# One decoder layer on one core: two head groups' values in one bank, causal masks by 32x32 products, and projections with both weight halves side by side

## The reference, cut to what matters

```
def attn(x):        # 16 heads of 8 features, causal
    q, k, v = x @ Wq.T, x @ Wk.T * scale, x @ Wv.T
    qk = einsum('bthd,bshd->bhts', q, k);  qk = where(causal, qk, -inf)
    qkv = einsum('bsdh,bhts->bthd', v, softmax(qk))
    return layernorm(qkv, gamma, beta) @ Wo.T
def xattn(k, v, q): # one head, 64 context rows
    return softmax((q @ Wq.T + bq) @ (k @ Wk.T).T * scale) @ (v @ Wv.T + bv) @ Wo.T + bo
def ffn(x):         # 8 experts, all of them, weighed by entmax gates
    return sum_e gate_e * (relu(x @ W1[e] + b1[e]) @ W2[e] + b2[e])
x = x + attn(layernorm(x)); x = x + xattn(ctx, ctx, layernorm(x)); x = x + ffn(layernorm(x))
```

## Time and profile before

| | us |
|---|---|
| median of 3 runs | 703.99 |
| lowest and highest | 702.42, 704.47 |
| the profiled execution | 702.24 |
| its span, first to last instruction | 700.5 |

### The profile page before, as it was taken

The page is one execution under the profiler, slowest core; times in us unless marked ns, Lnnn a source line. Parts: engine busy times, 40 slices in busy tenths (PEclk is TensorE's granted clock), DMA queues, the critical chain, the costliest instruction groups (busy, mean ns, idle before and its releaser), DMA issues.

```text
span 700.5 us, 14922 instructions
## 1 busy us (share of the span) xinstructions
PE 677.0 (97%) x4858; PEld 491.3 (70%) x4858; DVE 458.7 (65%) x969; ACT 422.7 (60%) x810; POOL 359.4 (51%) x588
## 2 busy tenths in 40 slices
PE   5889999999999999999999999999999999999997
PEld 3455655777677776787777777787768767777775
DVE  3763577459954797369865796379845995565544
ACT  3348335875587547854676647854686458665453
POOL 6434144663466426564475437643576337554362
PEclk9999789999999999999999999999999999999999
DMA  4514200052006300260006200440006200600050
GB/s 141 194 32 113 91 2 19 8 133 91 3 19 138 109 3 17 54 169 21 17 1 153 90 2 17 104 140 2 17 20 146 78 2 3 142 14 1 16 120 16
DMA packets 35299, 43.03 MB, mean 61 GB/s; under 512 B 2738, under 2 KB 18750, under 8 KB 35262
## 3 DMA queue, kind: packets, MB, share of 16 engines
q1 hardware_dynamic: 35262, 42.55, 22.6%
HBM read 10.04 MB, written 2.10 MB: 17 GB/s over the span
## 4 chain that ended last, share of the span: by engine, by line
PE 77%; DVE 10%; issue 6%; ACT 5%; SPq 1%; DMA 1%; POOL 0%; DVEq 0%; ACTq 0%; POOLq 0%
PE h_ps L936 9%; PE y_ps L936 7%; PE h_ps L938 7%; PE h_ps L937 7%; PE y_ps L938 7%; PE y_ps L937 7%; DVE negmax L1507 4%; PE sbuf_s L1015 3%; PE sbuf_m L1029 3%; PE sbuf_s L1029 3%; PE sbuf_s L997 3%; PE sbuf_s L992 3%; PE sbuf_s L968 2%; DVE h_lo L1616 2%; PE sbuf_s L936 1%
## 5 line engine op out<-in xcount | busy, mean ns | idle before, releaser
L1616 DVE SCALAR_TENSOR_TENSOR h_lo<-h_ps,h_hi 128x512 fp32r<-128x512 f32 x256 | 174.2, 685 | 158.9 <-ACT h_hi L1340 157.7
L1340 ACT ACTIVATE h_hi<-h_ps 128x512 fp32r<-128x512 f32 x256 | 152.4, 599 | 111.0 <-PE h_ps L938 106.0
L807 POOL TENSOR_SCALAR_AFFINE_SELECT prob<-prob 128x512 f32<-128x512 f32 x128 | 80.0, 641 | 133.4 <-ACT prob L1321 131.0
L1507 DVE TENSOR_REDUCE negmax<-sbuf_s 128x4 f32<-128x1024 f32 (+1 forms) x96 | 113.3, 1218 | 12.0 <-PE sbuf_s L997 10.3
L936 PE MATMUL y_ps<-h_lo,w_hi 128*128 128x512 f32 x255 | 109.4, 429 | 3.4 <-ACT y_sb L1349 2.3
L936 PE MATMUL h_ps<-fT_lo,w_hi 128*128 128x512 f32 x256 | 110.9, 433 | 1.5 <-DVE fT_lo L1482 0.9
L1321 ACT ACTIVATE prob<-sbuf_s 128x768 f32<-128x768 f32 x128 | 99.5, 812 | 15.6 <-PE sbuf_s L1015 14.8
L938 PE MATMUL h_ps<-fT_hi,w_hi 128*128 128x512 f32 x256 | 101.2, 395 | 0.0
L937 PE MATMUL h_ps<-fT_hi,w_lo 128*128 128x512 f32 x256 | 101.1, 395 | 0.0
L938 PE MATMUL y_ps<-h_hi,w_hi 128*128 128x512 f32 x255 | 100.7, 395 | 0.0
L937 PE MATMUL y_ps<-h_hi,w_lo 128*128 128x512 f32 x255 | 100.7, 395 | 0.0
(11 more groups left out here) (412 smaller groups left out, 1136.0 us busy)
## 6 DMA issues: line engine op xcount, KB each, us to landing
gate_b<-gT SPq DMA_DIRECT2D x64, 256.0 KB, 4.9
stacks<-qk SPq DMA_DIRECT2D x48, 256.0 KB, 2.5
x_t<-in_x_dram SPq DMA_DIRECT2D x8, 256.0 KB, 2.8
gate_b<-in_L_ffn_W_dram SPq DMA_DIRECT2D x1, 2048.0 KB, 9.5
x_r<-in_x_dram SPq DMA_DIRECT2D x8, 256.0 KB, 4.0
out_dram<-sums SPq DMA_DIRECT2D x7, 256.0 KB, 4.4
prob<-in_ctx_dram SPq DMA_DIRECT2D x1, 512.0 KB, 4.1
prob<-in_L_ffn_b_dram SPq DMA_DIRECT2D x1, 512.0 KB
```

The source lines that it names most:

```text
L807: pool.affine_select(out=v, in_=v, compare_op=ALU.is_ge, fill=0.0, base=0, pattern=[[0, 2], [0, 2], [1, P]], channel_multiplier=-1).then_i ...
L1340: act.activation(h_hi[:, c % HB, :], h_ps[:, c % 2, :], ACT.Relu).then_inc(hhi_made, 1)
L1507: dve.tensor_reduce(negmax[:, tile, :].rearrange("p (j g) -> p j g", g=NG)[:, j:j + 2, gs], halves[buf].rearrange("p j (g s) -> p j g s", ...
L1616: dve.scalar_tensor_tensor(out=h_lo[:, c % HB, :], in0=h_ps[:, c % 2, :], scalar=0.0, in1=h_hi[:, c % HB, :], op0=ALU.max, op1=ALU.subtrac ...
```

## The change

It has four parts.

1. **Values.** `PV` takes two head groups (four steps a round instead of eight). The window of 32 value columns of the second group starts 16 columns earlier, so that its 9 used columns land 16 partitions further, and its products add to the first group's in the same bank (`values`). There are as many products as before. `attT` has half its columns, so each `BT` has 2 transposes instead of 4, and ACT has 4 copies a round instead of 8. `prob` has three buffers.
2. **Masks.** In rounds the identity product is done as 16 products of 32x32, one for each strip of rows and of columns, and touches only the 32x32 blocks on the diagonal: 128 or 64 columns. The blocks beyond it are masked by six more rows of `qs` and `ks`, which were idle in the 32-row stacks. POOL makes these rows (`cells`) and SP spreads them by 8 DMAs in phase 0, behind SC 15 and ahead of the second K (`spread_cells`). The products L992 carry them at their old size. Phase 0 keeps the old masks.
3. **Projections.** In rounds V and WO use `project_wide`: the activations' hi part by both weight halves side by side (256 columns), then the lo part by the weights' hi half (128 columns), 8 matmuls instead of 12. The two halves of the result are added when the bank is read: V by four reductions on DVE instead of one copy, WO by two additions instead of one. Phase 0 keeps the old form.
4. **Places.** All tables are laid anew, and `FILL` has 63 matmuls instead of 105: of these 22 instead of 45 stand in phase 0 from the first MAX of the second pair on. `pairs` on DVE moves from between MAX 9 and MAX 10 (dve=5.5) to behind MAX 11 (dve=6.5), and the statistics SZ 1 move in between MAX 5 and MAX 6.

```
+PG = 3
...
 A_STEPS = [
-    Step("PV", 0, "m", pe=1.02, act=1.01),
-    Step("PV", 1, "t", pe=1.03, act=1.02),
-    Step("SC", 4, "s", pe=2.01, act=2.01, pool=0.25),
...
+    Step("PV", 0, "m", pe=1.02, act=5.01),
+    Step("SC", 4, "s", pe=1.03, act=1.01, pool=0.25),
...
-    Step("XO", 0, "m", pe=28.02, dve=28.03),
-    Step("SA", 2, "-", dve=28.04, pool=6.5),
-    Step("NA", 2, "-", act=30.01),
-    Step("T3", 0, "m", pe=32.51, act=31.01, dve=31.02),
+    Step("SA", 2, "-", dve=28.04, pool=6.25),
+    Step("XO", 0, "m", pe=28.52, dve=28.03),
+    Step("NA", 2, "-", act=31.01),
+    Step("T3", 0, "m", pe=32.52, act=31.02, dve=31.02),
...
+        def spread_cells():
+            sp.wait_ge(cells_made, 5)
+            for j in range(NJ):
+                r = slice(ROWS * j + 11, ROWS * (j + 1), 4)
+                for a, dst in enumerate((qs, ks)):
+                    sp.dma_start(words(dst[r, :, :]).rearrange("p g (b s) -> p (g b) s", s=S),
+                                 cell_rows[11:ROWS:4, a, :].unsqueeze(1).to_broadcast([6, 2 * NG, S]))\
+                      .then_inc(cells_loaded, 16)
...
+        def project_wide(buf, t_hi, t_lo, w, ks=range(NT)):
+            for k in ks:
+                t = slice(k * P, (k + 1) * P)
+                o = side_by_side(buf)[:, k, :, :]
+                pe.matmul(o, t_hi[:, t], w, start=True, stop=False)
+                last = pe.matmul(o[:, 0, :], t_lo[:, t], w[:, 0, :], start=False, stop=True)
+            return last
...
+                if ph.f is not None:
+                    for c in range(NJ):
+                        rows = slice(CELL * c, CELL * (c + 1))
+                        for j in js:
+                            t = slice(CELL * j, CELL * (j + 1))
+                            diagonal = sbuf_s[rows, j, :].rearrange("p (g s) -> p g s", s=width)
+                            last = pe.matmul(diagonal[:, :, width - P + CELL * c:width - P + CELL * (c + 1)],
+                                             ident_bf[t, t], causal[t, 0:len(gs), t],
+                                             start=False, stop=True, skip_group_check=True)
...
-                pe.wait_ge(prob_made, ph.a * 16 + 2 * n + 2)
-                for first in (True, False):
-                    for j in range(NJ):
-                        o = dst[VW * j:VW * (j + 1), :]
...
+                b, u = divmod(n, 2)
+                for v in range(2):
+                    pe.wait_ge(prob_made, ph.a * 16 + 4 * n + 2 * v + 2)
+                    for first in (True, False):
...
+                            c = ((2 * u * NJ) + 2 * j + v) * VW - v * VW // 2
...
-                    for g in range(NG):
-                        last = pe.transpose(dst[:, g * P:(g + 1) * P], attT[:, b, g, k * P:(k + 1) * P], ident[:, :])
+                    for u in range(2):
+                        last = pe.transpose(dst[:, u * P:(u + 1) * P], attT[:, b, u, k * P:(k + 1) * P], ident[:, :])
...
+                    for k in range(NT):
+                        ins = dve.tensor_reduce(v_t[:, k, :, 0:D], side_by_side(buf)[:, k, :, :].rearrange("p a (h d) -> p h d a", d=D),
+                                                AX.X, ALU.add)
...
+                    mark(dve.tensor_tensor(x1[:, ks, :], x_r[:, ks, :], side_by_side(buf)[:, ks, 1, :], ALU.add))
+                    settle()
+                    dve.tensor_tensor(x1[:, ks, :], x1[:, ks, :], side_by_side(buf)[:, ks, 0, :],
```

More of the change, by code:

```diff
@@ new lines @@
+    Step("xwv", 0, "m", pe=2, act=2.25, dve=1.75),
+    Step("kp", 0, "v", pe=2.25, act=2, dve=2.5),
+    Step("V", 0, "y", pe=2.5, dve=2.25),
+    Step("cells", 0, "-", pool=2.75),
+    Step("w1r", 0, "-", act=2.75, pool=1),
+    Step("MAX", 0, "s", pe=2.75, dve=2.75),
+    Step("w1r", 1, "-", act=3, pool=1.25),
+    Step("MAX", 1, "t", pe=3, dve=3),
+    Step("w1r", 2, "-", act=3.25, pool=1.5),
+    Step("MAX", 2, "s", pe=3.25, dve=3.25),
+    Step("MAX", 3, "t", pe=3.5, dve=3.5),
+    Step("NZ", 1, "-", act=3.5),
@@ new lines @@
+    Step("w1r", 3, "-", act=3.75, pool=2),
+    Step("xwo", 0, "u", pe=3.75, act=2.5, dve=4.5),
+    Step("MAX", 4, "s", pe=4, dve=3.75),
+    Step("pairs", 0, "-", act=4, dve=6.5),
+    Step("MAX", 5, "t", pe=4.25, dve=4),
+    Step("SZ", 1, "-", dve=4.25, pool=0.75),
+    Step("MAX", 6, "s", pe=4.5, dve=4.75),
+    Step("MAX", 7, "t", pe=4.75, dve=5),
+    Step("MT", 0, "m", pe=5, dve=5.25, sp=0.75),
+    Step("MAX", 8, "s", pe=5.25, dve=5.5),
+    Step("wr", 0, "u", pe=5.5, act=5, dve=8),
+    Step("MAX", 9, "t", pe=5.75, dve=5.75),
@@ L711, in step @@
                           .then_inc(nm_cleared, 16)
+                    if ph.first:
+                        spread_cells()
                 if name == "GT":
@@ L919, in step @@
                     constants()
+                if name == "cells":
+                    cells()
             def body(ph):
@@ L986, in max_scores @@
                         pe.wait_ge(nm_cleared, pair * 32)
+                    if ph.first and pair == 1:
+                        pe.wait_ge(cells_loaded, 16 * CELL_DMAS)
                 gs, width = (range(NG), P) if kind == 0 else (range(2 * kind - 2, 2 * kind), S)
@@ L998, in max_scores @@
                                      start=False, stop=True, skip_group_check=True)
-                    if j == 1 and len(js) == NJ:
-                        last.then_inc(full["s"], 1)
                 return last
@@ L1021, in values @@
             def values(ph, n, dst):
-                b, g = divmod(n, NG)
-                pe.wait_ge(prob_made, ph.a * 16 + 2 * n + 2)
-                for first in (True, False):
-                    for j in range(NJ):
-                        o = dst[VW * j:VW * (j + 1), :]
-                        last = pe.matmul(o[:, 0:S] if first else o[:, P:S], v_t[:, 2 * b + (not first), g * NJ + j, :],
-                                         blocks(prob[:, n % 2, j, :], first), start=first, stop=True,
-                                         skip_group_check=not first)
+                b, u = divmod(n, 2)
+                for v in range(2):
+                    pe.wait_ge(prob_made, ph.a * 16 + 4 * n + 2 * v + 2)
+                    for first in (True, False):
+                        tile = v_t[:, 2 * b + (not first), :, :].rearrange("p h w -> p (h w)")
+                        for j in range(NJ):
+                            o = dst[VW * j:VW * (j + 1), :]
+                            c = ((2 * u * NJ) + 2 * j + v) * VW - v * VW // 2
+                            last = pe.matmul(o[:, 0:S] if first else o[:, P:S], tile[:, c:c + VW],
+                                             blocks(prob[:, (2 * n + v) % PG, j, :], first),
+                                             start=first and v == 0, stop=True, skip_group_check=not (first and v == 0))
                 return last
@@ L1227, in _ @@
             for w in range(2):
-                act.activation(stack_order(wT_hi[:, w, :]), sbuf_s[:, w, 0:P].rearrange("p (g k) -> p g k", g=NG), ACT.Copy)
+                for u in range(2):
+                    act.activation(stack_order(wT_hi[:, w, :], u), head_order(sbuf_s[:, w, 0:P], u), ACT.Copy)
             act.activation(wT_hi[:, 2, :].rearrange("p (h d) -> p h d", d=D),
```

421 lines of the change are left out of this document (216 added, 205 removed).

## The result

The changed kernel takes 685.23 us (median of 4 runs, 676.22 to 687.46), against 703.2 us for the kernel before: a ratio of 0.971, 95% interval 0.968 to 0.974. The forecast was 679.0 with a range from 667 to 694. One of the four, the profiled execution of 687.46 us, counts as a slow one, and the ratio and its interval are those of the other three, whose median is 684.60. The sign and the range hold. The forecast is 6 us too low, and two errors of opposite sign are in it: the rounds gained more than was forecast, and phase 0, which was to gain, lost.

What follows compares the result with a forecast made beforehand. PE's instruction stream was taken to bound the rounds. Six rounds save 17.0 us, the phase without projections 1.5 and phase 0 6.5, together 25.0 off 702.24; against the median that gave 679.0 us, range 667 to 694.

Steps and rivals of the forecast that it cites:

- fewer transposes, one visit fewer: In a round, eight transposes fewer save 0.88 us, and 7 instead of 8 visits to a tiled shape save 0.3.
- round's end and the rest: At a round's end, XO later and MT ahead of T3 use up 0.4 us to spare: new stall of 0.5 us.
- four sets of four: Masks in a MAX step: 16 small products, four side by side, cost 0.22 us (0.14 with 64 columns); low ends 0.05, 0.03.
- a gain of 6.5: Phase 0: `pairs` and statistics moved gain 2, less ACT work 2, fewer fillers 2.5; bounds 0 and 11 us.
- I leave the fall in and count no gain from it: Phase 0, 80 to 90 us: the granted clock's fall to 0.50 was expected to remain, priced at nothing.
- pricing 23 fillers as 2.5 us: Last third of phase 0: 23 fillers fewer at 0.22 us make 5 us, half counted since DVE becomes the next bound.
- The second rival: Phase 0 keeps its length because DVE or the granted clock sets it: 685.5 us, chance 0.14.
- The 60 cycles: Masks: by the skill's overhead rule 16 products take 0.40 us whatever their width; the sum would be some 8 us higher.
- Small products one behind the other: Rival on masks: small products do not overlap fully, 0.60 us a step, 694.6 us; chance 0.14 for this side of 686.
- The chains: Rival: PE's savings in rounds return as waits ahead of T3, T2 or value steps; only phase 0 gains: 697.5 us, chance 0.04.
- the one where both turn out well: Rival: masks at the low price and phase 0 at its upper bound: 663 us, partly so 668; chance 0.10.
- The slower one: Rival on masks: each 32x32 product costs 0.107 us with nothing side by side: 735 us, chance 0.05.

Runs made afterwards that it cites:

- the repeat's: The changed kernel run again unaltered, with its 63 fillers, against the kernel before: 685.77 us (682.42 to 686.62), ratio 0.976.
- 104 fillers: The changed kernel with 41 more constants' matmuls in phase 0, 104 instead of 63: 673.92 us, ratio 0.959 to the kernel before.
- its base: The changed kernel with 104 instead of 63 constants' matmuls, in which the mask products were then doubled: 673.92 us.
- 86: The kernel with 104 fillers less 18 that stood where full-size products are just ahead: 673.87 us, ratio 0.959 to the kernel before.

## Why the prediction was right and wrong

**A round, term by term.** Forecast 2.8 us, measured 76.93 - 73.52 = 3.41. By prices in the two traces, each from start to start (the last row is what remains):

| | forecast | measured | by an experiment |
|---|---|---|---|
| fewer transposes, one visit fewer | 0.88 + 0.3 | 1.18 | 0.90 (transposes, done twice) |
| masks | 1.4 | 1.8 | 1.7 (taken back) |
| V and WO | 0.75 | 0.9 | 0.75 (taken back) |
| round's end and the rest | -0.5 | -0.45 | |

The way of pricing held: three of the four terms were within 0.2 us. The term that was mis-sized is "four sets of four" for the masks, 0.22 and 0.14 us for 16 products. Done twice, they take 0.11 and 0.08 more; the low ends of 0.05 and 0.03 were nearer. The MAX steps were forecast at 1.1 and 0.86 and are at 1.00 and 0.81. With these and the 0.19 for a change of shape as it was, the sum gives 1.56 - 0.88 + 0.11 + 0.19 = 0.98 and 0.97 - 0.44 + 0.08 + 0.19 = 0.80, so the price of the change of shape fits too.

The first row sums all steps of a round with values, scores alone and transposes back: 12.69 us before, 11.51 after. The forecast of 0.91 us is what WO takes, so half an expert product was the right neighbour for one of 256 columns. What was too small is the price before: I had 1.28 us from the first product to the one behind, while from start to start WO took 1.35 and V 1.39. Taken back, the projections are worth 0.74 us a round and not 0.92. DVE then has 1.15 us less work (forecast 1.7), so at most some 0.2 us of DVE's bill is felt and the rest is hidden; which part is which was not tested.

The stall at the round's end was foreseen in size, 0.5, and half in place. I expected T3 and `fT_lo` late; `fT_lo` is, by 0.1 more than in the earlier trace rows, but the last MAX, by ACT, and MT, by the reduction behind that MAX, are later. In return the waits for ACT's copies of `y_ps` and `cp`, 2.1 us over the six rounds before, are no longer among the waits listed in the rounds. The prediction took the 2.3 us of the earlier trace rows for a sum inside the rounds; it is the whole run's.

**The phase without projections**: 1.5 forecast, 1.36 measured.

**Phase 0**: a gain of 6.5 forecast, a loss of 6.6 in the profiled execution, of 1.2 in the repeat's and of 3.4 by the estimate for the median. This is the step that failed, and the failing sentence is "I leave the fall in and count no gain from it", together with pricing 23 fillers as 2.5 us of time to be won. A filler was read as work only. In these runs it also decided the clock: with 29 more of them in and near the last third the granted clock there is 1.00 instead of 0.50, and the kernel 9.3 us faster. The earlier trace rows showed how near the fall was: at 0.50 with PE busy throughout, in a kernel that had 45 of them from there on. The second rival had the mechanism (PE with 42 fillers less, the clock stays down longer) and its time, 685.5, is where the median came out; but it was given 0.14, and the argument against it, that `pairs` had been in the chain, speaks of something else. Its first half, PE idle more often, is not what happened: PE was busy 98% of the long stretch. That its time was met is luck: the rounds gained 3.4 us more than was in it, and phase 0 lost 3.4 where that rival had it unchanged. That the median lies only 6 us from the forecast is in part the same luck. MAX 12, the first step with the second K, starts at 82.71 us without a wait, so the eight DMAs on SP cost nothing, as priced.

Was the rest of phase 0's term right? By the windows, as an estimate: a mean clock of 0.77 over 123.54 us is 2 x 0.23 x 123.54 = 57 us at half clock, one of 0.83 over 118.16 is 40. The same kernel, so 5.4 us for 17, or 0.32 us for each us at half clock. Taken down to none, the changed kernel's phase 0 would be 118.2 - 12.8 = 105.4, and the kernel before's, with 0.93 and so 16 us at half clock, 116.9 - 5.2 = 111.7. The difference is 6.3, near the 6.5 of the forecast. This goes beyond what was measured. With 104 fillers and no time at half clock phase 0 took 108.02 us, in the run with old masks, whose phase 0 is the same program:

```profile
0.00:108.02 108.02, 95.61 (x697) 57.89 (x698) 68.34 (x145) 53.13 (x106) 52.17 (x89) 1.00 0.31 98
```

Beside it the 109.53 with 3.4 us at half clock gives 0.44 us for each, so the 0.32 is rough; with 0.44 the difference above would be 9.3. All this makes it likely, not certain, that order and fewer fillers did shorten phase 0's work by what was said or more, and that the clock took that and more.

**The 60 cycles.** The 16 products of 32x32 take 0.11 us more when done twice, where I had estimated 0.40 us from the rule of some 60 cycles of overhead for a matmul (the Trainium skill, TensorEngine Tiling (Array Packing), Instruction Overhead). For products that share the array in 16 blocks this case's trace does not agree with that estimate: 0.11 us with 128 columns and 0.08 with 64 are under a third of it. The estimate put the products one behind the other. The measurement decides.

**The other rivals.** Small products one behind the other would have given MAX steps above their old price; these are below. The chains didn't hold the round: doubled transposes are paid in full. Of the one where both turn out well, the masks came near their low price and phase 0 did not come. The slower one, 0.107 us for each product, is off by a factor of 15.

## What to carry to other kernels

When a change removes instructions that compute nothing, ask first what they did for the engine's clock, and read the granted clock in windows next to them: where it is at half already while the engine is busy, the cover is thin. Price a step by the distance between starts around it, and an unknown one by doubling it in a run. A gain that the sum has at one place and the result has not may be there all the same, under a loss elsewhere; windows by phase tell the two apart.

## What the runs showed of the chip

- A change of 41 filler matmuls, some 9 us of PE's work if each took its 0.22 us, moves the time of the kernel by 12 us in the other direction. The clock of TensorE went to half with the engine busy 98 to 100% of the stretch; before the longest fall it had done products of 128 columns, and with more fillers of 512 columns among the steps it stayed at 2.4 GHz. How many are needed, and where at the least, no run here settles: 86 gave the same median as 104.
- The same kernel's executions differ by the clock: with 63 fillers from 676.22 to 687.46 us at mean granted clocks of 0.982 and 0.956. The repeat's six, 682.42 to 686.62, have 0.968 to 0.961. With 104 the spread is 2.3 us.
- In the run with doubled masks PE once stood still for 4.24 us with nothing that it waited for in the profile. From 335.0 to 338.4 us its clock was at half. The row, and that of the page on the DMA queue of the kind "instruction":

```profile
335.54 0.77 PE L978 MATMUL h_ps<-fT_lo,w_hi 128*128 128x512 f32 x1 [4.24 <-issue]
```

```profile
q8 instruction: 32, 0.52, 0.3%
```

  The product that takes its turn in 0.23 us elsewhere takes 0.43 there. This round was 77.97 us and the next, with the half clock in it, 75.29, where the one before was 74.06. That queue moved 32 packets in this run and 21 in its base. Two of the 32 start at 330.87 and 331.67 us, as PE stops, and the second took 2.0 us; the base has none between 249 and 556 us. Instructions that came late are a likely cause, but no run tests it.
- Sixteen products of 32x32, each in its own block of the array, take 0.11 us with 128 columns and 0.08 with 64, as doubling them shows.
